# Eight bf16 products of ones behind the values of pair 0 are replaced by 32 fp32 products of ones on row tiles of 32 rows, 128, 64 and 32 columns wide

## The reference, cut to what matters

```python
xn = _ln_last(x, ln1_g, ln1_b)
q = _conv(_conv(xn, q1, 0), q3, 1).reshape(B, HEADS, HW, d)
k = _conv(_conv(xn, k1, 0), k3, 1).reshape(B, HEADS, HW, d)
v = _conv(_conv(xn, v1, 0), v3, 1).reshape(B, HEADS, HW, d)
score = jnp.einsum('bhpd,bhpe->bhde', k, q) / scale
probs = jax.nn.softmax(score, axis=-1)
attn = jnp.einsum('bhpd,bhde->bhpe', v, probs)
x = _conv(attn, o_w, 0) + x
xn = _ln_last(x, ln2_g, ln2_b)
gate = jax.nn.gelu(_conv(_conv(xn, g1, 0), g3, 1), approximate=False)
info = _conv(_conv(xn, i1, 0), i3, 1)
```

## Time and profile before

| | |
|---|---|
| time of three runs | 211.99 us median, 209.85 to 212.32 |
| span of the profiled execution, first to last instruction | 210.1 us |
| time of the profiled execution itself | not listed; the median of the runs is 1.9 us above its span |
| mean granted TensorE clock | 0.989 of full speed |
| PE busy | 184.5 us, 88% of the span |
| DVE busy | 161.3 us, 77% |
| ACT busy | 119.4 us, 57% |
| POOL busy | 70.5 us, 34% |

### The profile page before, as it was taken

How to read it: one execution, slowest core, us unless ns; L and a number is a source line. 1 busy time by engine, 2 the same in 40 slices (tenths; PEclk the granted TensorE clock), 3 DMA queues, 4 the chain that set the end, 5 groups by cost and what they waited for, 6 DMA issues and landing times.

```text
span 210.1 us, 5374 instructions
## 1 busy us (share of the span) xinstructions
PE 184.5 (88%) x2158; PEld 104.0 (50%) x2167; DVE 161.3 (77%) x382; ACT 119.4 (57%) x251; POOL 70.5 (34%) x62
## 2 busy tenths in 40 slices
PE   1799879879986999899997999899799998899972
PEld 1349339333353756643576455743423345565741
DVE  6798799988768859599497986994928576992682
ACT  2175273655259461967692862775845583966850
POOL 7600803150310403660007613750044003670290
PEclk9999999978999999999999999999999999999998
DMA  6412031001501000001000040001001000000002
GB/s 199 80 57 58 2 100 50 3 0 37 163 0 50 3 5 10 3 3 39 0 3 0 3 147 13 6 3 46 4 6 47 3 0 10 8 5 8 5 2 103
DMA packets 10154, 6.75 MB, mean 32 GB/s; under 512 B 7248, under 2 KB 8496, under 8 KB 10128
## 3 DMA queue, kind: packets, MB, share of 16 engines
q1 hardware_dynamic: 9888, 5.82, 10.2%
q10 hardware_dynamic: 240, 0.58, 0.7%
HBM read 3.30 MB, written 1.05 MB: 21 GB/s over the span
## 4 chain that ended last, share of the span: by engine, by line
PE 53%; DVE 22%; ACT 12%; issue 5%; DMA 3%; POOL 1%; SPq 1%; DVEq 0%; ACTq 0%
PE ps L1455 20%; PE ps L1375 5%; PE ps L1368 5%; PE ps L1402 5%; PE ps L1498 4%; ACT xw L703 3%; ACT p_t L720 3%; DVE sh_in L316 3%; PE ps L1533 3%; DMA w3b<-in_w_gi 2%; ACT sh_x L608 2%; PE ps L1544 2%; DVE ln_out L968 2%; PE ps L1522 2%; PE ps L1587 2%
## 5 line engine op out<-in xcount | busy, mean ns | idle before, releaser
L1455 PE MATMUL ps<-sh_ln,w_gi 96*64 96x512 f32 x192 | 44.6, 615 | 1.7 <-DVE sh_ln L316 1.7
L473 POOL TENSOR_TENSOR ln_s<-ln_s,neg_half 128x16 f32<-128x16 f32 x7 | 20.4, 2909 | 55.5 <-DVE ln_s L947 55.5
L608 ACT ACTIVATE sh_ln<-ln_out 32x512 f32<-32x512 f32 (+2 forms) x46 | 25.6, 557 | 14.6 <-DVE ln_out L968 5.5
L1455 PEld LDWEIGHTS ps<-sh_ln,w_gi 96*64 96x64 f32 x192 | 15.4, 140 | 25.9 <-issue 25.8
L1402 PE MATMUL ps<-w_qk,sh_ln 128*128 128x128 f32 x192 | 23.2, 278 | 0.4 <-issue 0.4
L1402 PEld LDWEIGHTS ps<-w_qk,sh_ln 128*128 128x128 f32 x192 | 22.2, 192 | 1.9 <-DMA sh_ln<-ln_out 0.9
L1498 PE MATMUL ps<-sh_in,w_in 96*32 96x256 f32 x384 | 22.8, 380 | 0.0
L1368 PE MATMUL ps<-busy 128*128 128x512 bf16 x68 | 19.4, 419 | 1.3 <-issue 1.2
L608 ACT ACTIVATE sh_x<-x 32x496 f32<-32x496 f32 (+1 forms) x20 | 12.3, 616 | 9.2 <-DVE x L1093 9.0
L1498 PEld LDWEIGHTS ps<-sh_in,w_in 96*32 96x32 f32 x384 | 11.9, 109 | 10.3 <-issue 3.0
L498 POOL TENSOR_TENSOR omm<-ones,msk 128x512 f32<-128x512 f32 x4 | 7.1, 1780 | 22.6 <-DVE msk L1169 22.6
(11 more groups left out here) (142 smaller groups left out, 334.6 us busy)
## 6 DMA issues: line engine op xcount, KB each, us to landing
sh_ln<-ln_out SPq DMA_DIRECT2D x27, 64.0 KB, 2.1
x_res<-in_x SPq DMA_DIRECT2D x4, 256.0 KB, 2.8
out_x<-out_s SPq DMA_DIRECT2D x4, 256.0 KB, 2.0
x_norm<-in_x SPq DMA_DIRECT2D x3, 256.0 KB, 2.9
kc<-in_shape_consts ACTq DMA_DIRECT2D x1, 450.0 KB, 4.9
w3b<-in_w_gi SPq DMA_DIRECT2D x1, 288.0 KB, 5.0
x_norm<-in_x SPq DMA_DIRECT2D x2, 128.0 KB, 2.8
xm<-xm SPq DMA_DIRECT2D x8, 25.5 KB, 1.9
```

Source lines behind the costliest of these rows:

```text
L473: nc.gpsimd.tensor_tensor(ln_s[n][:, 3, :], ln_s[n][:, 2, :], neg_half[:, :], ALU.pow)\
L608: return nc.scalar.activation(o, i, ACT.Copy)
L1455: mm = nc.tensor.matmul(ps[EC * h:EC * h + EC, GI_BANKS[n], :], w_gi[:, dy, n % 2, :], xs[:, n // 2, y:y + H // 2, 0:W], start=(dy == 0), ...
```

## The change

The call of eight bf16 products ahead of `attn_out(0)` goes. In its place TensorE waits until GpSimd has filled `ones`, and runs fp32 products of 32 rows of `ones` (partitions 0 to 31, 32 to 63, 64 to 95 and 96 to 127 in turn), each of the four row strips into a PSUM bank of its own (1, 4, 5 and 7): first eight with weights of 128 columns and 512 columns of data, then eight with weights of 64 columns and 256 of data, then sixteen with weights of 32 columns and 256 of data. With narrower weights the products write strips of 64 or 32 partitions, `j` naming the strip.

```diff
+            def row_tiles(rounds, m, n):
+
+                for _ in range(rounds):
+                    for j in range(P // m):
+                        for r in range(R):
+                            rows = slice(C * r, C * r + C)
+                            nc.tensor.matmul(ps[m * j:m * j + m, (1, 4, 5, 7)[r], 0:n], ones[rows, 0:m], ones[rows, 0:n],
+                                             start=True, stop=True)
+
@@
             by_head(0)
             v_by_head(0, (1, 2))
-            stay_busy(8, 5)
+            pe.wait_ge(s_zero, 2)
+            row_tiles(2, P, BANK)
+            row_tiles(1, EC, BLK)
+            row_tiles(1, C, BLK)
             attn_out(0)
             stay_busy(5, 5)
```

## The result

| | before | after |
|---|---|---|
| median of 20 runs | 211.41 us (209.21 to 213.56) | 213.16 us (211.06 to 214.19) |
| ratio | | 1.0085, 95% interval 1.0058 to 1.0112 |
| span of the profiled execution | 210.1 us | 212.2 us |
| its own time | not listed | 214.03 us, 1.8 above its span |

The time lies in the range and within two per cent, but the interval does not hold 1: the 1.75 us between the medians want a cause.

A forecast was written before the change was run, and what follows sets the result against it. VectorE's unbroken work, then `gate_info(0)`, was taken to hold the end around the change. Removed and added products (1.73 and 2.99 us) reach nothing, so the median of 211.99 stays: 212.0 us, range 209.6 to 214.1.

The forecast's parts named there:

- The sum of the row tiles: Added fp32 products ahead of `attn_out(0)`: parts of 1.80, 0.43 and 0.43 us plus 0.33 for form changes, 2.99 us.
- rival 1: Row strips sharing columns take turns in the added products, `attn_out(0)` 8.1 us late: 218.7 or 217.0; chance 0.10 (everything in turn 0.04).
- rival 2: Column strips of one row strip don't run side by side, added products 4.7 us: 212.4, or 210.7 if clock keeps; chance 0.08.
- `attn_out(0)` late but covered: `attn_out(0)` starts at 28.59 in place of 28.47, 0.12 us late, within the time its reader leaves.
- The cushion of 1.43 us: `attn_out(0)` may be about 1.43 us late before the VectorE addition reading it at 31.06 moves.
- The clock at the place: No new reason for a clock fall at the added products, which fill 0.96 us of TensorE idleness.
- rival 3: Added products don't hold the clock, half speed somewhere in 28 to 42 us: 212.5, 210.8 or 213.7; chance 0.11.
- The clock falls in one place only: Reading of the earlier profile: clock falls only in the slices from 42 to 53 us, all else at full speed.
- No queue is passed by anything: Side-effect check of the edit: the new wait holds nothing, the banks are unread in this stretch, no queue is affected.
- nothing reaches the end: With all strips side by side, the delay at `attn_out(0)` leaves the kernel's end unmoved: 212.0, chance 0.66.
- Removing them alone is worth nothing: The eight bf16 products ahead of `attn_out(0)`, 1.73 us, lie wholly in 2.87 us that cost nothing.
- the better case (210.8): A clock fall in 28 to 42 us shortens idleness ahead of `gate_info(0)`, so the later fall could go: 210.8.

The follow-up runs named there:

- c4: Changed kernel with the first row-tile part at four rounds in place of two, stream 256 instructions longer than the kernel before: ratio 0.9968.
- Count only: Kernel before, its eight bf16 products kept and 56 tiny ones added behind them, 112 instructions more without row tiles: ratio 1.0085.
- aligned: Changed kernel with 77 tiny products for the five behind `attn_out(0)`, stream 256 instructions longer than the kernel before: ratio 1.0039, then 1.0016.
- half aligned: Changed kernel with four bf16 products near 101 us replaced by 76 tiny ones, stream a whole load longer only from there: ratio 1.0050.
- d2: Changed kernel with idle time ahead of `gate_info(0)` filled by more products, stream 256 instructions longer than the kernel before: ratio 0.9912, 210.22 us.
- d4: Kernel before with eight tiny bf16 products in place of the eight of 512 columns ahead of `attn_out(0)`: ratio 0.9939.

## Why the prediction was right, and what it missed

- *The sum of the row tiles.* Forecast 2.99 us, measured 3.24. The parts were right (row strips and column strips side by side, rival 1 and rival 2 out); the first step of a part is longer than a later one (in the first part 0.53 us, 26.42 to 26.95, in place of 0.43).
- *`attn_out(0)` late but covered.* Forecast 0.12 us, measured 0.38 more behind `mix` than before; the addition and `qk(1, 0)` didn't move. The cushion of 1.43 us was confirmed by c4: 2.2 us late gave 0.79 where 0.7 was expected for 2.1.
- *The clock at the place.* 1.00 through the row tiles and up to 45 us, so rival 3 didn't come. "The clock falls in one place only" was a misreading: the last digit of the clock in the earlier trace rows is a second fall, from 208.9 us to the end. No term rests on it.
- *"No queue is passed by anything", and nothing reaches the end.* This step failed. It weighed the 24 instructions more only by their time on TensorE, and not as 112 entries of a stream that is itself loaded in 256s. The range held the time because 1.75 us is small against it, and no term of the sum foresaw them; that is luck. So is part of the nearness of 212.0 to 213.16: the three runs that the forecast started from have a median 0.6 us above that of 20. Count only, aligned, half aligned and d2 show this cause: the count gives the loss without row tiles, and the row tiles give none that can be told from noise with the loads back in place. The Trainium skill, "Runtime: NRT & Kernel Launch", Instruction fetch mechanics, tells of blocks of 256 instructions that are loaded while the one before runs, at a cost mostly hidden. The block is what the trace has; hidden it is not everywhere, 1.41 us in the middle of the scores.
- *"Removing them alone is worth nothing."* Wrong: d4, which nearly does that, gains 0.6%. I had kept the products' effect on the clock out of that step, and had rival 3 give the better case (210.8) only to row tiles; the kernel with next to nothing there came out at 210.79.

Open: how a program load delays the halo. The packets of the halo and the load run at the same time in each late case and in no other, and in two of the three the last 23 of 384 packets, about a sixteenth, start as the load ends. That looks like one of the page's 16 DMA engines being held by the load, but the records don't name the engine, and no run tried it. And the aligned kernel's own ratio, 1.003 as the mean of two, doesn't exclude a remainder of some tenths of a per cent.

## What to carry to other kernels

Count what an edit adds to an engine's instruction stream, also where its time is hidden: past the edit every boundary between program loads moves, and a stretch of short products, or a transfer on the path, may now meet one. To test an edit by itself, bring the stream to the same length modulo 256 instructions. And when an idle TensorE costs clock, ask where the half-speed stretch falls: in this kernel filler belongs ahead of the work that sets the end, and filler ahead of hidden work may move the fall to where it hurts.

## What the runs showed of the hardware

- Products of 32 rows run side by side where they share columns, with a PSUM bank for each row strip (no run shares one): 16 records of 512 columns and 128 wide in about 1.9 us, and 32 records of 256 columns and 32 wide on all sixteen tiles in about 0.7 us.
- TensorE may stand still inside a run of products without waits, for 1.41 us, at instruction 194 above a multiple of 256 in the order of its trace, and goes on 2.4 to 2.5 us behind the start of the load (2.2 to 2.8 at the value products of the runs that stall there).
- A transfer of 25.5 KB between partitions landed in 2.3 to 3.1 us in place of 1.9 when such a load ran beside its packets, and in 1.9 when the load had ended by the first of them.
- The half-speed stretch was 3.4 us long in each trace that has one ahead of the end. It began 0.2 to 1.7 us behind the start of `gate_info(0)` in eight traces with 1.73 or 1.74 us of idle time ahead of it, at 66 us in a ninth, and not near 45 us in the five with 1.31 us or less.
